# Moving 96 stores from SyncE's queue to ScalarE's in an attention and mixture-of-experts kernel

## The reference, cut to what matters

```python
x = x + xattn(layernorm(x), ctx)          # values rounded to fp8 and back, then one product
h = layernorm(x)                          # (4, 512, 512)
q, k, v = rmsnorm(h) @ q_w.T, ...         # 16 query heads, 4 key/value heads, 128 wide
attn = softmax(causal(rope(q) @ rope(k).T * scale)) @ v
hidden = h + attn @ o_w.T
tok = rmsnorm(hidden, ffn_norm_w)
probs = softmax(tok @ gate_w.T)           # 8 experts, the best 2 of each token
eg, eu = tok @ wg[e].T, tok @ wu[e].T     # (352, 512) each
eo = (silu(eg) * eu) @ wd[e].T
x = x + hidden + sum over the chosen experts of weight * eo
```

## Time and profile before

| what | value |
|---|---|
| median of 3 runs | 1429.47 us (1425.65 to 1430.74) |
| the profiled execution: its time, its span | 1427.62 us, 1425.8 us |
| mean granted TensorE clock | 0.960 |
| busy: PE, PEld, DVE, ACT, POOL | 1263.3, 1018.8, 843.3, 716.4, 384.6 us |
| the units of the experts' weights | from 407 to 1012 us |
| end of the first stage, about | 1105 us |

### The profile page before, as it was taken

The page is one execution under the profiler, slowest core; times in us unless marked ns, Lnnn a source line. Parts: engine busy times, 40 slices in busy tenths (PEclk is TensorE's granted clock), DMA queues, the critical chain, the costliest instruction groups (busy, mean ns, idle before and its releaser), DMA issues. The chain is left out here.

```text
span 1425.8 us, 22860 instructions
## 1 busy us (share of the span) xinstructions
PE 1263.3 (89%) x6845; PEld 1018.8 (71%) x6845; DVE 843.3 (59%) x2480; ACT 716.4 (50%) x2290; POOL 384.6 (27%) x545
## 2 busy tenths in 40 slices
PE   1767899998999989979999899998989299999995
PEld 0455667787776767767777677787767289999995
DVE  7667876766886766568777566665643522232231
ACT  5446665564675556466656555564553122333321
POOL 0223221232332222222213131331320224333332
PEclk9888899999999999989999999999999599999998
DMA  3270324431355555727554754665222797887433
GB/s 97 74 281 22 119 104 178 170 153 63 148 161 178 177 191 185 244 81 212 179 180 151 226 182 159 200 220 186 63 84 89 239 334 209 245 250 205 76 60 37
DMA packets 89894, 228.50 MB, mean 160 GB/s; under 512 B 12272, under 2 KB 50032, under 8 KB 79536
## 3 DMA queue, kind: packets, MB, share of 16 engines
q1 hardware_dynamic: 77536, 201.86, 40.3%
q0 software_dynamic: 10848, 24.71, 9.5%
q10 hardware_dynamic: 1392, 0.47, 0.1%
HBM read 146.76 MB, written 80.24 MB: 159 GB/s over the span
## 5 line engine op out<-in xcount | busy, mean ns | idle before, releaser
L537 POOL TENSOR_TENSOR prob<-prob,rtotal 128x128 f32<-128x128 f32 (+2 forms) x192 | 118.3, 622 | 438.9 <-DVE rtotal L1283 412.5
L954 ACT ACTIVATE prob<-prob,bias 128x128 f32<-128x128 f32 (+3 forms) x256 | 144.8, 566 | 150.0 <-DVE prob L1277 149.3
L1277 DVE TENSOR_SCALAR_CACHE_REDUCE prob<-bank,nscale 128x128 f32<-128x128 f32 (+3 forms) x256 | 134.8, 544 | 143.1 <-PE bank L715 142.7
L679 PE MATMUL bank<-w_hi,hT_hi 128*128 128x512 f32 x480 | 175.4, 365 | 17.4 <-DVE rot L1242 17.4
L734 PE MATMUL bank<-pT,v 128*128 128x512 f32 (+3 forms) x512 | 175.1, 444 | 8.6 <-ACT pT L960 7.9
L960 ACT ACTIVATE pT<-bank 128x512 f32<-128x512 f32 (+3 forms) x256 | 102.6, 432 | 125.7 <-PE bank L723 125.5
L679 PE MATMUL bank<-w_hi,hT_lo 128*128 128x512 f32 x480 | 163.9, 341 | 0.0
L679 PE MATMUL bank<-w_lo,hT_hi 128*128 128x512 f32 x480 | 163.5, 341 | 0.0
L1587 PE MATMUL gu<-we,xT_hi 128*128 x624 | 156.2, 332 | 3.0 <-DVE xT_lo L1703 2.7
L514 POOL TENSOR_TENSOR r<-r,rot 128x640 f32<-128x640 f32 x60 | 100.2, 1671 | 188.4 <-DVE rot L1242 188.4
L713 PE MATMUL bank<-kT_hi,qT_hi 128*128 128x128 f32 (+3 forms) x256 | 103.0, 402 | 22.9 <-DVE prob L1277 22.8
(11 more groups left out here) (312 smaller groups left out, 2861.9 us busy)
## 6 DMA issues: line engine op xcount, KB each, us to landing
w_hi<-ws_scratch SPq DMA_DIRECT2D x24, 1024.0 KB, 5.2
w_lo<-ws_scratch SPq DMA_DIRECT2D x24, 1024.0 KB, 7.5
we<-wx_scratch SPq DMA_DIRECT2D x16, 1408.0 KB, 10.6
we<-wx_scratch SPq DMA_DIRECT2D x16, 768.0 KB, 8.4
stage<-in_wexp SPq DMA_DIRECT2D x64, 176.0 KB, 2.4
wx_scratch<-ehi SPq DMA_DIRECT2D x64, 176.0 KB, 2.6
wx_scratch<-stage SPq DMA_DIRECT2D x64, 176.0 KB, 2.6
stage<-in_wqkvo SPq DMA_DIRECT2D x40, 256.0 KB, 3.3
```

The source lines that it names most:

```text
L537: nc.gpsimd.tensor_tensor(p, p, rtotal[:, 4 * h + q:4 * h + q + 1].broadcast_to([P, KEYS[q]]), ALU.mult).then_inc(prob_ready, 1)
L679: last = nc.tensor.matmul(o, hT[a][:, k, t * P:(t + 1) * P], wkv(j, c, k) if kv else wq(j, c, k), start=(k == 0 and n == 0), stop=(k == KC ...
L954: nc.scalar.activation(p, p, ACT.Exp, bias=bias[:, 4 * h + q:4 * h + q + 1], scale=-1.0, accum_out=total[:, 4 * h + q:4 * h + q + 1]).then ...
L1277: nc.vector.tensor_scalar(prob[(G * it + h) % (LAG + 1)][:, P_AT[q]:P_AT[q] + KEYS[q]], bank[SC + q % 2][:, 0:KEYS[q]], nscale[it % 2][:, ...
```

## The change

The store of a unit's high half is no longer asked for by SP but by ACT, on ACT's own queue. In each head ACT issues it one instruction behind the one that made the half at places 1 and 2 (behind the exponentials that follow), and straight behind it at place 3. `units` is the same. Nothing else is changed: the buffers, their numbers, the semaphores' counts and the transfers' sizes stay.

```diff
             def save_exp(m):
                 e, (at, cols, _) = m // len(PIECES), PIECES[m % len(PIECES)]
-                sp.wait_ge(exp_hi, m + 1)
-                sp.dma_start(wx_dram[e, 0, :, at:at + cols], ehi[m % RING_E][:, 0:cols].bitcast(F32)).then_inc(ehi_saved[m % RING_E], 16)
                 sp.wait_ge(exp_lo, m + 1)
                 sp.dma_start(wx_dram[e, 1, :, at:at + cols], stage[(NRAW + m) % RING_W][:, 0:cols]).then_inc(elo_saved[(NRAW + m) % RING_W], 16)
...
+            def save_hi(m):
+                e, (at, cols, _) = m // len(PIECES), PIECES[m % len(PIECES)]
+                act.wait_ge(exp_hi, m + 1)
+                act.dma_start(wx_dram[e, 0, :, at:at + cols], ehi[m % RING_E][:, 0:cols].bitcast(F32)).then_inc(ehi_saved[m % RING_E], 16)
+
...
+                def save(h, place):
+                    for kind, m in units(it, h, place):
+                        if kind == "ew":
+                            save_hi(m)
+
                 for h in range(G):
                     s = G * it + h - LAG
                     exponentials(it, h, 0)
...
                         copy_p(s, 1)
                     fill(h, 1)
                     exponentials(it, h, 2)
+                    save(h, 1)
                     if s >= 0:
                         copy_p(s, 2)
                         copy_p(s, 3)
                     fill(h, 2)
                     exponentials(it, h, 3)
+                    save(h, 2)
                     if s >= 0:
                         hi_attn(s)
                     fill(h, 3)
+                    save(h, 3)
```

## The result

The change made the kernel faster: 1405.28 us median (1403.31 to 1409.96, 6 runs) against 1430.45 us (1425.65 to 1433.83, 6 runs) for the kernel before, a ratio of 0.9828 with a 95% interval of 0.9807 to 0.9849. The forecast was 1413, with a range of 1405 to 1427. The direction and the mechanism were as forecast; the size was 24 to 25 us in place of 16.7.

A forecast was written before the change was run, and what follows sets the result against it. PE bounds the kernel, busy 89% of the span, with 39.0 us idle in the experts' stretch. 14.7 + 5.0 - 3 = 16.7 us off 1427.62 gives 1410.9; the median, 1.85 above, makes 1412.8, said 1413, range 1405 to 1427.

The forecast's parts named there:

- Why the store lands late: High-half stores at (2, 2) and (2, 3): delayed by SP's order and the queue; one landed 7.7 us after issue, undisturbed 2.6.
- The high-half store at (2, 2): On ACT, issued about 2 us before SP's, landing at 511.3, so the unit at (3, 1) doesn't wait.
- The high-half store at (2, 3): On ACT; the unit at (3, 2), which needs it, is reached at 517.5 instead of 520.1.
- The worst price beside big loads: Slowest landing for an ACT store beside big loads, taken from a 6 KB ACT transfer that landed after 15.1 us.
- my signs of being wrong: Stores on ACT landing after 7 us or more, PE's same four stalls, or `prob` and `pT` waits of 25 us and more.
- the queue doesn't matter: Rival, chance 0.11: all stores land as late as before, ACT's stalls stay; 1429, at most 1429.5 + 3.
- What takes the wait's place: At (3, 2) ACT waits for the `stage` refill, 517.5 to 520.8; half 5.5 us earlier, PE's four stalls close, gain 14.7 us.
- the refill takes over: Rival, chance 0.19: refill or ACT 2 to 3 us later, stalls of 1.5 to 2.5 us stay in three places; about 1418.
- The clock: PE's granted clock no longer falls behind the three stalls above 4 us: 5.0 us more gain.
- The 96 issues on ACT: Issues of 0.45 us add 43 us to ACT, mostly hidden by waits; 3 us taken as exposed.
- The rival's mechanism: Rival "ACT's issues reach PE", chance 0.08: ACT's delays pass through DVE to PE, deciding from 44 exposed issues; slower, 1437.
- SP: SP has 41 us less to issue, worth nothing but 0.4 us, as it mostly waits for landings.

The follow-up runs named there:

- e1: Kernel before, all stores still on SP, but those of (2, 2) and (2, 3) asked for ahead of the big loads: 1405.81 us, ratio 0.981.
- e11: Kernel before, with ACT storing only the high half of (2, 3), 9 of 96, and SP the other 87: 1409.12 us, ratio 0.9853.
- e3: Kernel before, with ACT storing 78 high halves and SP still those of (2, 2) and (2, 3): 1431.99 us, ratio 0.9992.
- e6: Full change with each high-half store cut into 4 transfers of 32 partitions, 384 issues on ACT: 1430.78 us, ratio 1.0002.
- e5: Full change with each high-half store cut into 2 transfers of 64 partitions, 192 issues on ACT: 1412.76 us, ratio 0.9876.

## Why the prediction was right, point by point

- **Why the store lands late**: right. Of the two causes that it named, SP's order and the queue, a better order on SP is enough for the time (e1 against the full change: 0.981 and 0.9828). It does not take the two causes apart: in e1 the store of (2, 3) was still asked for behind the refill, and what it gained was its place ahead of two big loads in the same queue.
- **The high-half store at (2, 2)**: landed in time, as forecast: asked for at 505.41, 2.1 us before SP's first big load, it took 2.1 us.
- **The high-half store at (2, 3)**: no wait, as forecast, and it landed after 7.4 us, at 515.8, ahead of the 517.6 at which ACT came to the unit that needs it. The worst price beside big loads was an estimate of mine: no run shows how the 15.1 us of the 6 KB transfer carry over to a store of this size. What the runs show is that the five such stores took 6.9 to 8.4 us and landed only 0.3 to 1.5 us before SP's; how the 16 engines share their time between the two queues is not shown. The late landing did no harm because the step needed only the early issue. Stores on ACT of 7 us or more were also one of my signs of being wrong; they came, and the time was right all the same, so the sign was badly chosen. The rival "the queue doesn't matter" has e1 for it (0.981 without ACT's queue), and yet its time was wrong: what ACT saved was not issuing time but the store's place behind a wait and big loads.
- **What takes the wait's place**: right in kind, and the gain was right, but not the wait. The refill paces ACT at (3, 2), 0.76 us in the worked iteration against 3.3 forecast, and 3.5 us in five waits of the whole stretch, where I had named three or four of 2 to 4 us. ACT reached the unit 9.9 us behind the half of (2, 3), not 7.8: I had taken off the whole first stall of 3.04 us, and 2.4 us of it came back as waits of `pT` for PE (2.07 and 0.37). The refill landed 0.5 us sooner, so the half ran 6.0 us earlier, against 5.5 forecast. PE's stall closed in all four episodes, 14.8 us of waits gone against 14.7 forecast. The rival "the refill takes over" did not come about.
- **The clock**: mis-sized. I counted the three falls behind the long stalls, 5.0 us. The runs show the clock as a share of full speed only, and this size with it: a mean of 0.66 in 5 us, with 0.50 inside the fall, is 3.4 us at half clock, which costs 1.7 us. In this profile four more were missing, 1.7 us each by the same rows, 11.8 us in all; PE's busy time fell by 10.6 us, where I had named it about unchanged. This is most of the miss. Those four were in part luck: the second profile of the change has one of them, and e11, without long stalls, three.
- **The 96 issues on ACT**: mis-sized, 3 us forecast, nothing that can be told from zero measured (e3: -0.1% with 78 of them, and the interval reaches from -0.3% to +0.1%). An issue takes 0.33 us and at places 1 and 2 runs inside the exponentials, which I had it follow. The rival's mechanism is real, but with one issue a unit hardly any was exposed; it took 384 issues, with ACT held up by them for 59 us in all (48.2 for `aT_hi`, 7.9 for `pT`, 2.9 for `prob`), to lose the gain (e6).
- **SP**: 41 us less to issue were worth nothing, as forecast; e3 has four fifths of that relief and no gain.

With PE's idle time and busy time as measured, 14.2 + 10.6 - 0 in place of 14.7 + 5.0 - 3, the sum is 24.8 us, the shortening of the stretch (they add up to it by definition). The two misses, in the clock and in the issues, went the same way. One sum of a rival was off by little: the refill's case, 1429.5 - 16.7 + 6, is 1418.8, not 1418.5.

## What to carry to other kernels

When an engine waits for a store, look at what stands ahead of the store's issue in the issuing engine's program, before looking at bandwidth: here 9 stores of 96 were asked for behind a wait for another transfer and behind two big loads. Moving those alone to ACT gave nearly all of the time (e11); leaving them on SP, but ahead of the big loads as those of (2, 2), gave as much (e1). An issue on a computing engine was free where a longer instruction of that engine covered it (0.33 us inside exponentials of 0.65 us), and cost once there were more issues than cover (384 of 0.44 us in e6, 1430.78 us against 1405.28), though the engine was idle for 40% of the stretch. Count the clock too when a stall of PE closes, but with a wide range: here 14 us of idle time and about 10 us of clock went together, and more than half of the latter stood at short pauses of PE, at which the clock fell in some executions and not in others.

## What was not expected of the hardware

- A transfer asked for by ACT behind an activation did not wait for that activation's end: it went out 0.04 us after the half that it waited for (502.21 for 502.17), inside the exponentials that had started at 502.04, and a `dma_start` of 0.33 us (128 partitions) cost ACT nothing there. Cut to 64 partitions it took 0.50 us at the median and up to 2.1 (e5), cut to 32 still 0.44 (e6), so smaller transfers did not make shorter issues.
- A store of 176 KB on ACT's queue, beside 2 MB on SP's, landed after 7.4 us; one on SP's own queue, asked for at the same moment behind the same loads, after 7.7 us.
- The granted clock fell to half for 3.4 us at four short pauses of PE (1.2 to 2.4 us) in both profiles of the kernel before, at none or one of them after the change, but at three in e11, which has none of the long stalls, and at two in e3, which has them all.
